# An FFN with adapters and 16 experts on one core: the last four output stores are issued from ScalarE instead of GpSimd

## The reference

```python
w = weight[adapter_ids]
h = jnp.einsum('bsi,boi->bso', x, w)
gu_s = x2 @ shared_w_gate_up.T
g_s, u_s = jnp.split(gu_s, 2, axis=-1)
shared_out = jax.nn.silu(g_s) * u_s @ shared_w_down.T
logits = x2 @ gate_w.T
probs = jax.nn.softmax(logits, axis=-1)
topk_vals, topk_idx = jax.lax.top_k(probs, TOP_K)
...
gu = jnp.einsum('th,eih->eti', x2, w_gate_up)
g, u = jnp.split(gu, 2, axis=-1)
act = jax.nn.silu(g) * u
out_e = jnp.einsum('eti,ehi->eth', act, w_down)
moe_out = jnp.einsum('eth,te->th', out_e, combine)
return (moe_out + shared_out).reshape(orig_shape)
...
x = x + _L0_ffn_ref(_L0_cond_ref(x, ...), ...)
```

## Time and profile before

| | |
|---|---|
| device time, median of 3 runs | 1130.09 us (1129.95 to 1130.22) |
| profiled execution: span from first to last instruction | 1131.0 us |
| PE busy | 1108.0 us, 98% of the span |
| DVE, ACT, POOL busy | 567.2, 475.7, 166.3 us |
| mean granted TensorE clock | 0.993 of full speed |
| DMA | 247.45 MB, mean 219 GB/s |

### The profile page before, as it was taken

The page is one execution under the profiler, slowest core; times in us unless marked ns, Lnnn a source line. Parts: engine busy times, 40 slices in busy tenths (PEclk is TensorE's granted clock), DMA queues, the critical chain, the costliest instruction groups (busy, mean ns, idle before and its releaser), DMA issues.

```text
span 1131.0 us, 16957 instructions
## 1 busy us (share of the span) xinstructions
PE 1108.0 (98%) x5250; PEld 917.4 (81%) x5251; DVE 567.2 (50%) x638; ACT 475.7 (42%) x602; POOL 166.3 (15%) x250
## 2 busy tenths in 40 slices
PE   8999999999999999999999999999999999999996
PEld 7788888888887888888888887788888888888885
DVE  6556555436764445654644544444462355344452
ACT  6556564433233455665645555532331223132210
POOL 1112121000011111111111111041003110032041
PEclk9999999999999999999999999999999999999998
DMA  9787786521256568787786887364256534464264
GB/s 352 291 317 273 266 307 228 198 75 75 89 210 224 191 227 312 252 309 255 293 307 221 310 309 274 124 247 154 92 225 234 213 111 197 156 223 162 79 223 148
DMA packets 40931, 247.45 MB, mean 219 GB/s; under 512 B 4994, under 2 KB 5122, under 8 KB 30594
## 3 DMA queue, kind: packets, MB, share of 16 engines
q1 hardware_dynamic: 14530, 154.15, 36.0%
q0 software_dynamic: 20032, 71.31, 18.4%
q10 hardware_dynamic: 6336, 21.56, 5.1%
HBM read 201.39 MB, written 49.81 MB: 222 GB/s over the span
## 4 chain that ended last, share of the span: by engine, by line
PE 95%; issue 1%; ACT 1%; DVE 1%; DMA 1%; ACTq 0%; DVEq 0%; SPq 0%
PE bank L516 30%; PE bank L518 30%; PE bank L517 29%; PE bank L684 3%; PE bank L537 1%; PE bank L529 1%; PE bank L717 1%; DMA raw<-cond_w 1%; ACT w_split_sb L798 0%; DVE w_split_sb L1050 0%; ACTq L248 0%; ACT y_out L798 0%; ACT hT_hi L798 0%; DVE tile_hT L1050 0%; DVE e_act L1336 0%
## 5 line engine op out<-in xcount | busy, mean ns | idle before, releaser
L1050 DVE TENSOR_TENSOR w_split_sb<-raw,w_split_sb 128x2048 fp32r<-128x2048 f32 (+3 forms) x152 | 259.2, 1728 | 92.9 <-ACT w_split_sb L798 92.0
L798 ACT ACTIVATE w_split_sb<-raw 128x2048 fp32r<-128x2048 f32 (+3 forms) x152 | 218.2, 1463 | 95.3 <-PE bank L518 85.3
L516 PE MATMUL bank<-hT_hi,w_split_sb 128*128 128x512 f32 x512 | 200.0, 391 | 0.9 <-ACT y_out L798 0.9
L517 PE MATMUL bank<-hT_lo,w_split_sb 128*128 128x512 f32 x512 | 199.4, 389 | 0.0
L518 PE MATMUL bank<-hT_hi,w_split_sb 128*128 128x512 f32 x512 | 199.4, 389 | 0.0
L516 PE MATMUL bank<-w_split_sb,tile_hT 128*128 (+1 forms) x312 | 125.7, 403 | 3.8 <-issue 2.6
L518 PE MATMUL bank<-w_split_sb,tile_hT 128*128 (+1 forms) x312 | 122.5, 393 | 0.0
L517 PE MATMUL bank<-w_split_sb,tile_hT 128*128 (+1 forms) x312 | 122.5, 393 | 0.0
L516 PEld LDWEIGHTS bank<-hT_hi,w_split_sb 128*128 128x128 f32 x512 | 96.1, 188 | 21.2 <-issue 1.3
L517 PEld LDWEIGHTS bank<-hT_lo,w_split_sb 128*128 128x128 f32 x512 | 96.1, 188 | 19.9
L518 PEld LDWEIGHTS bank<-hT_hi,w_split_sb 128*128 128x128 f32 x512 | 96.1, 188 | 19.9
(11 more groups left out here) (149 smaller groups left out, 1529.1 us busy)
## 6 DMA issues: line engine op xcount, KB each, us to landing
raw<-sh_gu_w SPq DMA_DIRECT2D x16, 2048.0 KB, 9.0
raw<-exp_gu_w SPq DMA_DIRECT2D x16, 2048.0 KB, 8.7
raw<-cond_w SPq DMA_DIRECT2D x14, 2048.0 KB, 8.6
y_dram<-y_out ACTq DMA_DIRECT2D x39, 512.0 KB, 6.1
raw<-sh_down_w SPq DMA_DIRECT2D x8, 2048.0 KB, 7.9
raw<-exp_down_w SPq DMA_DIRECT2D x16, 1024.0 KB, 7.3
h_dram<-h_row POOLq DMA_DIRECT2D x32, 256.0 KB, 6.0
x_raw_sb<-xT SPq DMA_DIRECT2D x7, 1024.0 KB, 11.0
```

The source lines that it names most:

```text
L516: nc.tensor.matmul(dst, lhs[0], rhs[0], start=first, stop=False)
L517: nc.tensor.matmul(dst, lhs[0], rhs[1], start=False, stop=False)
L798: return nc.scalar.activation(dst, src, ACT.Copy)
L1050: return nc.vector.tensor_tensor(dst, src, hi.bitcast(F32), ALU.subtract)
```

## The change

The four stores of quarter 3 and the waits for their landing move from the end of GpSimd's program to the end of ScalarE's. Each store still waits for the same value of `comb`; it raises a new semaphore `q3_out[m]` instead of `rows_out[m]`.

```diff
@@ -205,6 +205,7 @@
         rows_in = [sem(f"rows_in{m}") for m in range(QM)]
         rows_out = [sem(f"rows_out{m}") for m in range(QM)]
         out_half = [sem(f"out_half{m}") for m in range(QM)]
+        q3_out = [sem(f"q3_out{m}") for m in range(QM)]
 
         rt_step = sem("rt_step")
         rt_z = sem("rt_z")
@@ -496,13 +497,6 @@
             wait(su_mm, FB * QUARTERS)
             for m in range(QM):
                 fetch((QUARTERS - 1) * QM + m, m, acc_dram, m * P, rows_q3, 16)
-            for m in range(QM):
-                wait(comb, QM * (QUARTERS - 1) + m + 3)
-                pool.dma_start(out[(QUARTERS - 1) * QTOK + m * P:(QUARTERS - 1) * QTOK + (m + 1) * P, :],
-                               rows_q3[m][:, :]).then_inc(rows_out[m], 16)
-
-            for m in range(QM):
-                wait(rows_out[m], 16 * QUARTERS)
 
 
         @block.tensor
@@ -1037,6 +1031,13 @@
                 shared_quarter(qq, False)
             shared_quarter(QUARTERS - 2, True)
 
+            for m in range(QM):
+                act.wait_ge(comb, QM * (QUARTERS - 1) + m + 3)
+                act.dma_start(out[(QUARTERS - 1) * QTOK + m * P:(QUARTERS - 1) * QTOK + (m + 1) * P, :],
+                              rows_q3[m][:, :]).then_inc(q3_out[m], 16)
+            for m in range(QM):
+                act.wait_ge(q3_out[m], 16)
+
 
         @block.vector
         def _(dve):
```

## The result

The changed kernel takes 1122.26 us (median of 5 runs, from 1120.8 to 1124.23) against 1130.22 us before (5 runs, 1129.95 to 1131.29). The ratio is 0.9927, 95% interval 0.9916 to 0.9939: 0.73% faster, 8.3 us of 1130.09 (6.9 to 9.5).

What follows compares the result with a forecast made beforehand. TensorE is busy 98% of the span, but GpSimd's DRAIN ends the program. Last DRAIN from 1130.8 to 1123.5 us, other costs hidden: 1130.09 - 7.25 = 1122.8 us, 0.64% faster; range 1122.2 to 1125.6.

Steps and rivals of the forecast that it cites:

- What bounds the end: Block's end: GpSimd's DRAIN of 8972 ns ends last at 1130.8 us, by 7.3 us; the waits view wrongly names TensorE.
- The DRAIN begins at the last gather and is hidden: GpSimd's end: DRAIN starts at 1105.6 us, 16.2 us earlier, hidden before SyncE's 1123.5 if under 17.9 us long.
- three bounds for its length: GpSimd's DRAIN ends at 1114.6 us counted from its start, 1120.8 from the last landing, 1117.0 from the last issue's end.
- ScalarE's stores: ScalarE's end: four stores, 0.34 us issue each, hidden; the fourth lands in 2.6 to 2.9 us; earlier first two cost 0.
- Rival D: Last gather lands late behind ScalarE's stores, making the kernel slower: 1132.5 us if it takes 23 us; chance 0.03.
- The tail's term: Program's end: last DRAIN moves from 1130.8 to 1123.5 us, span 7.25 us shorter.
- 0.3 for run to run: Allowance in the range's lower end, 1122.2 us, beside 0.3 us less for closing events and landing.
- The offset of 0.9 us: Whole kernel: median of the runs lies 0.9 us below the profiled span, taken as unchanged by the change.
- rival C's second variant: GpSimd's DRAIN is long only under the profiler, so nothing is gained; about 1129.8 us, chance 0.08 for both variants together.
- B: GpSimd's DRAIN with gathers in flight lasts 17.9 to 25.2 us and ends the program; about 1126.5 us, chance 0.05.
- C's first: DRAIN's end tied to something other than its start; 1129.3 us if the cost moves to ScalarE; chance 0.08 for both variants.
- The two pages: Counted against the forecast: by the first the sum would be 0, by the second nothing could be won at the end.

Runs made afterwards that it cites:

- late DRAIN: The changed kernel with GpSimd also waiting at its program's end for VectorE's last add, so its DRAIN begins later; ratio 1.0005 to the kernel before.
- early DRAIN: The kernel before with a DRAIN added on GpSimd between its last gather and its four stores, which stay on GpSimd; ratio 0.9946.
- two masked kernels: The changed kernel and the kernel before, each with the expert's number that engines wait against masked with 31; ratios 0.9947 and 1.0013 to the kernel before.
- three stores: The kernel before with only the fourth store moved to ScalarE and three left on GpSimd; ratio 0.9956.
- the added DRAIN at 701 us: The kernel before with one more DRAIN on GpSimd, ahead of its first fetch; ratio 0.9959.
- the one at 215 us: The kernel before with one more DRAIN on GpSimd, behind the first stage's 56 stores; one run of 1128.52 us, no ratio.
- small kernel: Computation left out: SyncE copies x to the output, GpSimd issues 0 to 164 scratch stores; its DRAIN took 41 ns without a DMA, 3.2 us behind 164.

## Why the prediction was right, and where it was off

- **What bounds the end** was right: GpSimd's DRAIN, against the name that the view of waits gives. The late DRAIN gives the whole gain away with the stores on ScalarE, and the early DRAIN wins it with the stores on GpSimd.
- **The DRAIN begins at the last gather and is hidden** was right. It ended at 1114.2, by the prediction's first bound 1114.6, in an execution in which all of the end lies 1.0 us earlier; against that it took 0.6 us longer than forecast. Its row stands at 1102.6 with 11.6 us, not near 1105.6 with 9, for the reason given above. Of the three bounds for its length, the first holds: from where GpSimd has nothing left to do (its last issue over and its last wait past) it takes 8.9 to 9.9 us in these kernels. The two that count from a landing or from an issue that ended earlier were refuted by the late DRAIN, which began 15.8 us behind the last issue and took 9.2 us all the same.
- **ScalarE's stores** were priced right: 2.6 us to landing in the median, nothing queued behind them. The first, in the crowded stretch, took 6.8 us, and SyncE's slowest store there 6.5 us instead of 4.8. Neither delayed anything: the last combine starts 4.83 us ahead of the last add, as before. Rival D's gather was never late.
- **The tail's term** was right: 7.25 us forecast, 7.3 measured from trace to trace, 7.5 by the two masked kernels.
- **The step that failed is the lower end of the range**, its term "0.3 for run to run". It was taken from three runs within 0.27 us. The paired ratio gave 8.3 us, to 1121.8 us on the old median, 0.4 under the range's 1122.2; the median of the five runs, 1122.26, lies just inside. The ratio's own interval is 1.3 us to either side, four times the term: five runs of the changed kernel spread over 3.4 us, and the 60 ordinary runs of the kernel before that were taken with the experiments range from 1126.78 to 1134.98. By that spread the forecast's 7.25 us and the measured 8.3 can't be told apart, and the masked pair gave 7.5. The tail's term was not mis-sized; the 1.0 us by which the two traces differ beyond it lies ahead of the first `fetch`, where the change does nothing, and fell on the changed kernel's side by luck. On the other side the range had 2.8 us of room.
- **The offset of 0.9 us** between span and median was misread, without effect on the forecast, in which it cancels. In every run of the large kernels on record the time is 1.5 to 1.6 us above the span, not below: 1124.23 and 1122.7 for the changed kernel's profiled execution, and the same in those 60 runs of the kernel before. So the profiled execution of before, with a span of 1131.0, was a long one of about 1132.5 us (an estimate; its own time is not on record). The argument against rival C's second variant, that span and median agree within 0.9 us, rested on that reading; the runs of the late and the early DRAIN refute the variant without it.
- **Rivals B and C.** B (the DRAIN lengthens with gathers in flight) has a grain of truth: in the five traces in which it begins so, behind 160 DMAs, it takes 9.5 to 9.9 us from the end of the last issue, against 9.2 us behind the same 160 with nothing in flight; B needed 17.9. C's second variant (only under the profiler) is refuted by the measured times of the late and of the early DRAIN. C's first (the price moves to whoever stores) is refuted by ScalarE's DRAIN of 8 ns.
- **The two pages.** The Trainium skill, "DMA: Bandwidth & Descriptors", section "Issuing engines are not separate DMA queues", says that DMAs run on the same 16 DMA engines whoever issues them; the runs agree, with a tail of 3.3 us by SyncE's stores and 3.1 by ScalarE's. The 7.3 us are not in the transfers. The Trainium skill, "VectorE: DVE Perf Modes", section "The DRAIN you can't avoid", gives about 12 ns for such DRAINs on all engines; the runs agree for SyncE and ScalarE (7 and 8 ns), and not for GpSimd: 41 ns in the kernel in which it had issued no DMA, thousands in the others.

What stays open: what GpSimd does in those 82 ns for each DMA; and how many are settled on the way in the large kernel. Before, 164 DMAs left a debt of (8972 - 41) / 82 = 109, with three stores 108, and with 160 in the late DRAIN 112; the added DRAIN at 701 us, behind 104 DMAs, took 6.7 us from the end of the last issue, where 82 ns each would give 8.5, and the one at 215 us, behind 56, took 6.7 too, where they would give 4.6. The mixture of stores and gathers in loops does not follow the simple count of the small kernel. Nor is it shown what makes the first 740 us differ from one execution to the next.

## What to carry to other kernels

Look at the instructions behind the program's last line, not only at the chain of work: an engine whose program ends late can hold all others there, and the one named by the view of waits need not be it. If GpSimd has issued many DMAs, let its program end early, or put a DRAIN of its own into a stretch where it idles, so that the debt (82 ns for each DMA, where the count held) is paid under cover; late stores then go through SyncE or ScalarE, or stay on GpSimd if they are few. And take run to run from many runs or several traces: three close times were no measure of it here. Two traces are compared best from an event that the change can't have moved, as the first `fetch` here: from there on they agree within 0.06 us.

## What the runs showed of the hardware

GpSimd's DRAIN is not free and not fixed: 41 ns without a DMA, and, with all of them landed, 82 ns more for each DMA issued since the last DRAIN (84 at 4 of them), at 4, 60, 64, 108 and 128 of them, whether of 128 KB or of 64 KB, 128 rows or 16. Behind 160 to 164 DMAs the count fails: 8.9 to 9.2 us in the large kernels, where it would give 13.2 to 13.5. The debt doesn't fade with time (9.2 us, 15.8 us after the last issue). With a DMA in flight a DRAIN took 6.7 us behind 56 DMAs and behind 104. In one small kernel a gap of 3.19 us in the issue came behind 128 DMAs, and the DRAIN at the end, behind 164, took 3.2 us instead of 13.5. DRAINs of SyncE and ScalarE behind their DMAs took 7 and 8 ns.
